# Two convolution and two mixing layers in a chain: the first mixing moved onto 32-row tiles, two examples ahead

## The reference

```
x = x + M0 x + b0        first mixing: M0 (128x128) depends on the example
x = x + conv(x, w1) + c1 9 taps along time, 4 groups of 32 channels
x = x + M2 x + b2        second mixing
x = x + conv(x, w3) + c3
```

## Time and profile before

| | |
|---|---|
| median of 3 runs | 2628.59 us (2625.79 to 2630.22) |
| profiled execution | 2628.2 us, of which span 2626.3 us |
| mean granted TensorE clock | 0.997 |
| PE busy | 2602.8 us, 99% |
| DVE busy | 2440.0 us, 93% |
| ACT busy | 2010.8 us, 77% |
| POOL busy | 791.5 us, 30% |
| DMA queue | 489.39 MB, 58.6% of 16 engines |

### The profile page before, as it was taken

The page is one execution under the profiler, slowest core; times in us unless marked ns, Lnnn a source line. Parts: engine busy times, 40 slices in busy tenths (PEclk is TensorE's granted clock), DMA queues, the critical chain, the costliest instruction groups (busy, mean ns, idle before and its releaser), DMA issues.

```text
span 2626.3 us, 107053 instructions
## 1 busy us (share of the span) xinstructions
PE 2602.8 (99%) x42610; PEld 1812.2 (69%) x42610; DVE 2440.0 (93%) x3218; ACT 2010.8 (77%) x3480; POOL 791.5 (30%) x1039
## 2 busy tenths in 40 slices
PE   8999999999999999999999999999999999999997
PEld 6667766776677667666766776677767766776765
DVE  7999999999999999999999999999999999999995
ACT  6777777777777777777777777777777777777774
POOL 0223222322332333223322332233223322322232
PEclk9999999999999999999999999999999999999999
DMA  4556655665666556555555665566556655655554
GB/s 147 182 183 195 194 182 185 194 192 182 187 192 194 182 187 196 189 182 187 195 190 182 190 199 183 182 194 196 181 182 193 197 181 182 196 194 182 184 185 159
DMA packets 228045, 489.80 MB, mean 187 GB/s; under 512 B 47016, under 2 KB 129072, under 8 KB 195376
## 3 DMA queue, kind: packets, MB, share of 16 engines
q1 hardware_dynamic: 228016, 489.39, 58.6%
HBM read 205.04 MB, written 150.99 MB: 136 GB/s over the span
## 4 chain that ended last, share of the span: by engine, by line
PE 96%; DVE 2%; SPq 1%; ACT 0%; issue 0%; DMA 0%; DVEq 0%; ACTq 0%
PE ps L376 41%; PE ps L355 28%; PE ps L327 14%; PE ps L342 13%; SPq L225 1%; DVE y L705 0%; DVE m_sum L657 0%; DMA m_parts<-mixed 0%; DVE prod L652 0%; ACT y_full L516 0%; PE ps L273 0%; SPq L215 0%; ACT y L516 0%; DVE y L699 0%; DVE xp L677 0%
## 5 line engine op out<-in xcount | busy, mean ns | idle before, releaser
L376 PE MATMUL ps<-y,conv_parts 32*128 32x512 f32 x18432 | 1129.5, 392 | 2.5 <-DVE y L705 1.2
L376 PEld LDWEIGHTS ps<-y,conv_parts 32*128 32x128 f32 x18432 | 925.5, 184 | 177.7 <-issue 46.9
L705 DVE TENSOR_TENSOR y<-y_full,y 128x512 fp32r<-128x512 f32 x1020 | 913.5, 956 | 115.3 <-ACT y L522 115.1
L516 ACT ACTIVATE y_full<-ps,bias 128x512 f32<-128x512 f32 x1018 | 654.0, 692 | 276.5 <-PE ps L327 170.6
L355 PE MATMUL ps<-y_full,conv_raw 32*32 32x512 f32 (+1 forms) x16384 | 754.1, 596 | 1.6 <-DVE y_full L738 1.6
L822 POOL COPY bias<-bias_table 128x4 f32 (+3 forms) x512 | 183.9, 373 | 1812.9 <-DMA o_ch<-o_ph 1660.0
L828 POOL COPY o_t<-o_ch 128x512 f32<-128x512 f32 x508 | 633.3, 1364 | 13.6 <-DMA o_ch<-o_ph 13.6
L522 ACT CAST y<-y_full 128x512 fp32r<-128x512 f32 x1020 | 559.0, 633 | 0.4 <-DVE y_full L738 0.4
L355 PEld LDWEIGHTS ps<-y_full,conv_raw 32*32 32x32 f32 (+1 forms) x16384 | 274.9, 117 | 409.3 <-issue 407.1
L571 ACT ACTIVATE o_ph<-ps,bias 128x512 f32<-128x512 f32 x381 | 234.3, 687 | 227.0 <-PE ps L376 227.0
L327 PEld LDWEIGHTS ps<-xp,m_own 128*128 128x128 f32 x1524 | 277.7, 189 | 163.0 <-issue 57.3
(11 more groups left out here) (61 smaller groups left out, 130.2 us busy)
## 6 DMA issues: line engine op xcount, KB each, us to landing
x_t<-x SPq DMA_DIRECT2D x128, 1024.0 KB, 5.4
o_ch<-o_ph SPq DMA_DIRECT2D x2032, 64.0 KB, 2.0
out<-o_t SPq DMA_DIRECT2D x127, 1024.0 KB, 4.1
m_parts<-mixed SPq DMA_DIRECT2D x512, 128.0 KB, 2.6
mixed<-m_own SPq DMA_DIRECT2D x128, 128.0 KB, 1.7
conv_raw<-conv_w SPq DMA_DIRECT2D x2, 768.0 KB, 9.8
mix_sb<-mix_w SPq DMA_DIRECT2D x2, 576.0 KB, 7.4
out<-x_t SPq DMA_DIRECT2D x4, 256.0 KB, 4.2
```

The source lines that it names most:

```text
L376: ins = nc.tensor.matmul(ps[:, bank + t, :], conv_parts[layer][rows, w, s - DENSE[0], :], src[rows, a, p_in, q:q + N], start=first, stop=f ...
L516: nc.scalar.activation(dst, src, ACT.Identity, bias=bias[layer][:, k % WIDTH[layer]:k % WIDTH[layer] + 1]).then_inc(done[layer], 1)
L705: nc.vector.tensor_tensor(dst, full, high.bitcast(fp32), ALU.subtract).then_inc(low_set[layer], 1)
```

## The change

TensorE's order becomes: dense and sparse first convolution of i, sparse and dense second convolution of i - 1, first mixing of i + 2, second mixing of i. The first mixing takes the form of the second: x is loaded so that a row tile of 32 holds a quarter of the time, and a matrix by groups is used, which also goes through DRAM. The first three examples (`WHOLE`) keep the old form. PSUM banks are no longer exchanged: 4 to 7 serve the first convolution and the first mixing, 0 to 3 the second convolution and the second mixing, with exceptions at both ends.

```diff
+            def first_mix(j):
+
+                pe.wait_ge(m_in[0], 16 * G * (j - WHOLE + 1))
+                pe.wait_ge(low_set[1], 4 * (j - 1))
+                for g in range(G):
+                    pe.wait_ge(x_low_set, nth(j - 1, g))
+                    for n, (m, a) in enumerate(PASSES):
+                        first, final = g == 0 and n == 0, g == G - 1 and n == len(PASSES) - 1
+                        for q in range(G):
+                            rows = slice(CG * q, CG * (q + 1))
+                            ins = nc.tensor.matmul(ps[:, first_bank(j) + q, :], m_parts[0][rows, g, m, :], xp[rows, a, g, :],
+                                                   start=first, stop=final)
...
@@ TensorE, step
-                    sparse(1, y1_full, own, NARROW + WIDE)
+                    sparse(1, y1_full[odd], conv1_bank(i), False, free1)
...
-                if has(i, inner, 1):
-                    sparse(3, y3_full, other, WIDE + NARROW)
...
-                elif has(i, inner, -1):
-                    first_mix(i + 1, own, free0)
                 if has(i, inner, 1):
+                    pe.wait_ge(full_set[2], 4 * i)
+                    sparse(3, y3_full, third, True, free3)
                     pe.wait_ge(low_set[2], 4 * i)
-                    dense(3, y3, other, lambda t: None, lambda: None)
+                    dense(3, y3, third, False, free3)
+                if has(i, inner, -2) and (inner or i > 0):
+                    first_mix(i + 2)
                 if has(i, inner, 0):
-                    second_mix(i, own, free2)
+                    second_mix(i, free2)
```

SyncE loads x in four DMAs of 256 KB (from the fourth example on), stores and loads a matrix for each mixing, issues the moves by phase instead of by group, each phase with a wait for GpSimd's copy of the phase before it in time, and stores the output of i - 1 in the same step:

```diff
+                for q in range(G):
+                    sp.dma_start(x_t[CG * q:CG * (q + 1)],
+                                 x[j].rearrange("(g c) (q n) -> q c g n", g=G, q=G)[q]).then_inc(x_in, 16)
...
+            def shuffle(j, p, first, matrix=None):
+                if p == 0:
+                    sp.wait_ge(phases_set, 3 * j + 3)
+                    sp.wait_ge(phases_last, j + 1)
                 if not first:
+                    sp.wait_ge(in_time_set, nth(j - 1, p))
+                for g in range(G):
+                    if g == 1 and matrix is not None:
+                        sp.wait_ge(stored[2], 16 * matrix + 16)
                     sp.dma_start(o_ch[CG * g:CG * (g + 1), p, :], o_ph[CG * p:CG * (p + 1), g, :]).then_inc(shuffled[p], 16)
...
@@ SyncE, step in the loop
+                    sp.wait_ge(x_low_set, 4 * (i + 2))
+                    load_x(i + 3)
+                    shuffle(i - 1, 0, opening)
+                    shuffle(i - 1, 1, opening)
+                    store_matrix(0, i + 3)
+                    shuffle(i - 1, 2, opening)
+                    store_matrix(2, i + 1)
+                    load_matrix(0, i + 3, False)
+                    shuffle(i - 1, 3, opening, i + 1 if inner else None)
+                    load_matrix(2, i + 1, False)
+                    sp.wait_ge(in_time_set, 4 * i)
+                    sp.dma_start(out[i - 1], o_t[:]).then_inc(out_done, 16)
```

ScalarE, VectorE and GpSimd get new orders. The fourth quarter of the first mixing's evacuation goes from ScalarE to VectorE (`full_0_last`), and `y1_full` gets a second buffer. GpSimd waits for one phase's moves at a time and makes that phase's copy, with a bias copy between:

```diff
@@ ScalarE, step
-                    high_1(i, own_banks(odd), False)
-                    full_0(i + 1, own_banks(odd))
-                    high_0(i + 1)
-                output(i - 1, other_banks(odd), not inner and is_last(i), not inner and i == 1)
-                    full_2(i, own_banks(odd), False)
-                    high_2(i, False)
+                high_2(i - 1, not inner and i == 1)
                     x_high(i + 2)
+                    high_1(i, False)
+                    high_0(i + 1, 1 - odd)
+                output(i - 1, not inner and is_last(i), not inner and i == 1)
+                    full_0(i + 2, odd)
+                    full_2(i, False)
@@ VectorE, step
+                low_2(i - 1)
+                    x_low(i + 2)
+                    low_1(i)
+                    low_0(i + 1, 1 - odd)
+                    output_last(i - 1, not inner and i == 1)
+                    matrix(0, i + 3)
+                    full_0_last(i + 2, odd)
+                    halves(0, i + 3)
                     matrix(2, i + 1)
                     halves(2, i + 1)
@@ GpSimd, step: wait phase 0, bias 1, copy 0; wait phase 1, bias 0, copy 1;
@@ wait phase 2, bias 2, copy 2; wait phase 3, bias 3, copy 3
```

More of the change, by code:

```diff
@@ L237, in step @@
             def step(i, inner, odd):
-                if has(i, inner, 2):
-                    sp.wait_ge(in_time_set, 4 * (i - 1))
-                    sp.dma_start(out[i - 2], o_t[:]).then_inc(out_done, 16)
-                moves = has(i, inner, 1) and (inner or not is_last(i))
-                if moves:
-                    shuffle(i - 1, 0)
-                if has(i, inner, -1):
-                    store_matrix(i + 1)
-                if moves:
-                    for g in range(1, G):
-                        shuffle(i - 1, g)
-                if has(i, inner, -1):
-                    load_matrix(i + 1, False)
                 if has(i, inner, -3):
@@ L341, in second_mix, with sparse @@
                                 wait_bank(p)
-                            ins = nc.tensor.matmul(ps[:, bank + p, :], m_parts[rows, g, m, :], y2[rows, a, g, :], start=first, stop=final)
+                            ins = nc.tensor.matmul(ps[:, second_bank(j) + p, :], m_parts[2][rows, g, m, :], y2[rows, a, g, :], start=first, stop=final)
                             if final:
                                 ins.then_inc(mm[2], 1)
-            def sparse(layer, src, bank, lots):
+            def sparse(layer, src, bank, begins, wait_bank):
+                lots = WIDE + NARROW if begins else NARROW + WIDE
                 for r, units in enumerate(lots):
@@ L843, in step @@
                     set_bias(1, i + 1)
-                if has(i, inner, -2):
-                    pool.wait_ge(full_set[0], 4 * (i + 2))
-                    set_bias(0, i + 2)
+                if moves:
+                    in_time(i - 1, 0)
+                if not inner and i == 0:
+                    pool.wait_ge(full_set[0], 6)
+                    pool.wait_ge(full_last, 2)
+                    set_bias(0, 2)
+                moved(1)
+                if has(i, inner, -3):
+                    pool.wait_ge(full_set[0], 3 * (i + 3))
+                    pool.wait_ge(full_last, i + 3)
+                    set_bias(0, i + 3)
+                if moves:
+                    in_time(i - 1, 1)
+                moved(2)
+                if has(i, inner, -1):
+                    pool.wait_ge(full_set[2], 4 * (i + 1))
+                    set_bias(2, i + 1)
+                if moves:
+                    in_time(i - 1, 2)
+                moved(3)
                 if has(i, inner, 0) and (inner or i > 0):
```

311 lines of the change are left out of this document (173 added, 138 removed).

## The result

| | before | after |
|---|---|---|
| median | 2627.19 us | 2728.16 us (2723.86 to 2728.5) |
| ratio | | 1.0381, 95% interval 1.0367 to 1.0396 |
| profiled execution / span | | 2723.9 / 2722.1 us |
| PE, DVE, ACT, POOL busy | 99, 93, 77, 30% | 97, 87, 70, 31% |
| DMA queue | 489.39 MB, 58.6% | 571.38 MB, 77.8% |

The change makes the kernel 3.8% slower, about 100 us. Single executions slower than the rest (6123.64 us of the kernel after, 4861.53 of e8, 2656.4 of e9) count in no ratio and have no cause shown; the medians include them, and the range above leaves the first out. The forecast had the sign (48%), but 2728 lies above its range (2598 to 2705).

A forecast was written before the change was run, and what follows sets the result against it. SyncE's queue was to become the bound: 18.6 us of issues plus stops of 0.95 and 0.65 make 20.2, taken as 20.3 against 20.14; over 125 steps +20 on 2628.2 gives 2648 us, range 2598 to 2705.

The forecast's parts named there:

- TensorE's part: TensorE's matmuls per period: first mixing saves 0.16 us, dense second convolution 0.06, so 20.14 falls to 19.92.
- That SyncE's queue decides: SyncE's DMA queue: 18.6 us of issues plus stops exceed PE's 19.92, so it sets the period; 0.41 likely.
- the sum of the stops on top: SyncE's queue: 18.6 us of issues plus stops of 0.95 and 0.65 give 20.2 us a period, taken as 20.3.
- part of the stretch: GpSimd's fourth copy, slowed by VectorE: lengthens SyncE's wait from 0.95 towards 1.35 us, taking the period from 20.2 to 20.3.
- (a): SyncE before the output store: waits for the last moves to land and GpSimd's fourth copy, 0.95 us, 1.35 if stretched.
- (b): SyncE behind the 1 MB output store: x's second quarter is held, taken as 0.65 us, bounds 0 and 1.98.
- the likeliest case: SyncE's queue sets the period, 20.3 us: 2648 us, chance 0.41, own range 2636 to 2705 (period 20.2 to 20.75).
- What would be late next: PE first waits at the second mixing for its DRAM matrix, about 2 us late; then moves and output evacuation.
- PE keeps the bound: Rival: x's loads are not held behind the store, SyncE needs 19.55 and PE 19.92, giving 2601 us; chance 0.35.
- VectorE as the bound at 20.05: Rival: VectorE's 17.5 us plus 2.25 contention and 0.3 hand-overs; within the 20.0 to 20.08 case, 2611 to 2620, chance 0.07.
- The long hold: Rival: SyncE's queue held longer, x's quarters by 1.98 us (2798) or the fourth copy by a product (2804); chance 0.07.
- The opening and the end: One more first mixing before the loop and one less at the end: put at nothing, within 5 us.

The follow-up runs named there:

- e8: Kernel after, each of the four loads of x bringing only a quarter of its bytes (later examples partly older): 2655.43 us, ratio 1.0104.
- e9: Kernel after, with the first mixing's matrix loads issued by ScalarE instead of SyncE: 2637.68 us, ratio 1.0008.
- e2: Kernel after, with the next example's four x loads ahead of the output store in SyncE's queue: 2629.47 us, ratio 1.001.
- e4: Kernel after, with twelve already met waits added to SyncE's queue in each step, no bytes moved: 2751.12 us, ratio 1.0463.
- e10: Kernel after, with ScalarE issuing the first mixing's matrix loads and the next x ahead of SyncE's output store: 2622.45 us, ratio 0.9978.
- e12: e10 with GpSimd's output bias copied before its wait for the last phase's moves: 2617.17 us, ratio 0.9964.
- e1: Kernel after, with the 1 MB output store issued by GpSimd behind its fourth copy instead of by SyncE: 2638.52 us, ratio 1.0038.
- e7: Kernel before, with x loaded in four DMAs of 2 KB rows instead of one of 8 KB rows: 2627.26 us, ratio 1.0.
- e5: Kernel after, with the four x loads issued by ScalarE ahead of its output evacuation instead of by SyncE: 2953.92 us, ratio 1.1235.

## Why the prediction was right and wrong

**TensorE's part: right in sum, wrong in one term.** The forecast period was 19.92; the least of the pieces is 19.94. The first mixing saved what the earlier trace rows gave, 2.97 to 2.80. The dense second convolution gained nothing, where 0.06 was forecast: 4.26 start to start before, averaged over the trace, and 4.26 after. The 4.35 against 4.19 that I read as a price of changing shape is how the chain of the earlier trace rows cuts the pieces, at modelled ends; start to start over the whole trace the dense first convolution takes 4.31 and the dense second 4.26. Another 0.04 was gained by the first, 4.31 to 4.27, which no term named. The Trainium skill's rule (TensorEngine Tiling, Key Properties) that a change of mode drains the engine gave 0.16 saved and 19.98; between entering this stretch from the whole array and from 32x32 matmuls no difference shows.

**That SyncE's queue decides: right**, by e2 (no waits, and the queue's sum is the period), by e4 (what the waits in the queue don't take up shows in full) and by e9 and e10 (other relief of the queue takes the loss back too). Its 18.6 us of issues, counted from the earlier trace rows, measured 18.5.

**The step that failed is the sum of the stops on top, "20.2 us, 20.3 with part of the stretch".** Three terms were too small. (a) The wait for the fourth copy: 0.95 taken and 1.35 kept as an end, 1.36 measured. The stretch was not on the copy, as I had it from the earlier trace rows, but on the bias copy ahead of it, which was in no term: it is held for 0.47 us on average, and without that the 0.95 would have been near. So the end at 1.35 came near by luck. (b) The hold behind the store: 0.65 taken, 0.9 measured, because the third quarter of x is held as well (0.22). (c) The branch of SyncE's loop, 0.24 a step, was in no term; in the kernel before it had lain in slack. The three make 0.9, and the issues were 0.1 under their sum: together 0.8 over the 20.2, 0.66 over the 20.3, and 0.66 x 122 steps = 80 us, which is 2648 to 2728. The ends kept for (a) and (b), 1.35 and 1.98, were wide enough; the likeliest case's own range stopped at a period of 20.75, and what lay beyond was given some 0.1.

**What would be late next: half right.** The first wait is at the second mixing for its matrix, as forecast (0.49 and 0.87 in the rows; start to start 0.55 over 2.80 on average). SyncE's wait for the copy stayed at 1.3 us a step (169.6 over 127), where under 1 was my sign. The waits for x (258.8 us) and the bias (342.7 us) were not forecast as a loop that feeds back: late x, late lows, held GpSimd, longer queue. e8 shows it, 73 us under the time of after with x's bytes cut and the bias copy back at 0.20 us.

**The rivals.** PE keeps the bound fell, and with it the 2601: even e12, with four issues fewer in SyncE's queue, reaches 2617. VectorE as the bound at 20.05 fell for the change, but it was the right next one: it holds part of e10's period. The long hold (1.98) did not come for x, which came at 0.9; it did come in e1, 2.3 us, with the moves behind x. The Trainium skill (SBUF — State Buffer, Who interferes with whom) calls the port that the two engines share an exclusive lock, with the second to issue blocked until the first has finished. I had given that rule little weight because the earlier trace rows showed both engines sharing four by four (from 1305.55 to 1311.19 together, 5.64 us and not the 5.3 that I put, still under 6.5 in turn). The rows of after agree with it: the bias copy stands until an L769 has ended. How many it stands for differs. A copy that starts during the third of the four waits for the fourth too, 58 times of 114; at 1334.06 in the rows of after a bias copy that starts during the third of four L741, VectorE's lows of x, is through after 0.59 us, with that one's end. The runs don't show what decides it.

**The opening and the end** at nothing: right. (20.96 - 20.15) x 122 = 99 us is the whole difference.

**Open.** Why the issues behind a 1 MB store are held, and why by 0.9 us where x follows, 1.5 where moves follow, and 2.3 where x and moves follow a store by GpSimd, was not settled: e8 excludes x's bytes, e7 its form where slack covers it, and nothing was tried on the store's own form. The other half of e10's 0.18 us, and the spread of e9 over 44 us, have no cause shown. Why x in e5 meets the matrix in every second step alone was not looked into.

## What to carry to other kernels

Before a change moves transfers onto a queue, add up that queue's issues, branches and met waits for one period as for an engine, and put beside the sum every wait inside it for another engine's work: once the slack is gone, each counts in full. Then ask what can stand in the place of the wait: putting the four loads of the next x ahead of the output's store was worth about 98 us here with no work saved. A load moved to another queue must be looked at for what will be in flight beside it: 0.5 MB in a quiet place was free, 1 MB beside a matrix that TensorE needs cost some 225 us, in waits and in the clock that fell behind each wait.

## What was not expected of the hardware

A 128x4 copy on GpSimd took 0.20 us alone and up to 1.1 us when it started during four back-to-back two-input instructions of VectorE, which kept their 2.48 us; in the earlier trace rows, where GpSimd's copies had started first, both paid, VectorE's four with 4.75 us for 2.50 and the copies with 5.27 for 3.98. After TensorE had stood for 3.4 us, its next 48 matmuls were granted 0.59 of the clock on average and took 5.15 us instead of 3.00 (e5). On SyncE, a pass of the loop cost 0.48 us beside its issues, a met wait about 0.03 us, a 64 KB move between SBUF partitions 0.59 us of issue (0.63 start to start) and a 256 KB load of x 0.32 us (0.50): the larger transfer is the cheaper issue.
